# Last chunk of a gated state scan: key scaling, read-out sums, gates and the tensor engine's filler products change places

## The chip, the cores and the metric

The kernel runs on one core of a Trainium2 chip. The metric is the device time of one execution in microseconds (us). A core has a tensor engine (PE, with its weight loads shown apart as PEld), a vector engine (DVE), a scalar engine (ACT), GpSimd (POOL) and a queue engine for transfers (SP). Each takes its own instructions strictly in the order written; between engines only counting semaphores hold an instruction back.

## The reference

Four layers run on x of 4 rows (batch entries) by 1024 positions by 256 numbers, each followed by a residual sum and a layer norm: retention attention, a feed-forward block with four wide products, a gated state scan, and a small mixing layer. The change touches the scan and the mixing layer of the last chunk:

```python
# scan: for each position t, 32 blocks of 8; here the batch is the "step"
k_norm = k_t / (norm(k_t) + 1e-06)
retrieved = einsum('bnij,bnj->bni', S, k_norm)
S = tanh(S + outer(v_t - retrieved, k_norm))
Sq = einsum('bnij,bnj->bni', S, q_t)
out = Sq * silu(Sq)
# mixing layer
xr = mu_r * x + (1 - mu_r) * x_prev
xk = mu_k * x + (1 - mu_k) * x_prev
out = sigmoid(xr @ W_r.T) * (relu(xk @ W_k.T) ** 2 @ W_v.T)
```

The scan's first axis is what the other layers call the batch, so it has four steps (rows 0 to 3), each on 1024 positions that are independent of each other.

## The kernel before

The 1024 positions are cut into 8 chunks of 128, one position per partition. Attention runs first. Then a software pipeline (`schedule`) takes one chunk after another through the feed-forward layer, the scan of the chunk before and the mixing of the one before that. Behind it stands `finish()`, written once for each engine, with an order of instructions written out by hand: the last feed-forward product, the scan and mixing layer of the last chunk (number 7), and the mixing layer of chunk 6. `finish()` starts at about 1041 us of the profiled execution and is all that the change touches; nothing of it issues a transfer but the four stores at the end.

Names within `finish()`:

- A step's state is 128 partitions by 2048 numbers and is handled in two halves, (step, 0) and (step, 1), of 1024 numbers each.
- DVE: `guess_of(rows)` sums a row's squared keys (L2422) and makes a first guess of the inverse root. `scaled_keys(n, rows)` takes the reciprocal of the norm (L2436) and multiplies the keys (L2438). `next_state(s, hf)` computes state times keys (L2452), a sum (L2454), a difference (L2456), an outer product (L2458) and the added state (L2460). For the second halves of steps one and two, `state_delta` (L2467, L2471, L2473) and `state_added` (L2479) leave the outer product to POOL. `read_sum` (L2487) sums a product of state and query that POOL made; `last_read` makes that product on DVE (L2500) and sums it (L2502). `gate_rows` (L2529, L2532) gates the read-out and adds the residual for two rows, front (0 and 1) or back (2 and 3). `mixed_pair` (L2561, L2565) ends the mixing layer of a pair of rows.
- POOL: `key_root(n, rows)`, 13 small operations (L2084 to L2095), refines the inverse root. `read_q` (L2108) multiplies state and query, `outer_product` is L2116, `mix_weights` L2071, `added_mean` L2123 and `added_root` L2130, L2056 and L2058 (mean and inverse root of a layer norm, with sums from ACT).
- ACT: `key_value_row(b)` squares keys (L1818) and copies keys and values out of PSUM (L1821), `query_row(b)` copies the query (L1826) and frees the one PSUM bank of all queries. `state_tanh` is L1834, `gate_parts` L1839 and L1840, `add_rows` and `add_squares` L1847 and L1858, `scaled_rows` L1798, `turned_pair` L1867 and L1870, `key_acts` L1892 and L1894, `mix_gates` L1901.
- PE: the mixing layer runs on four pairs of rows, numbered 0 to 3: chunk 6 rows 0 and 1, chunk 6 rows 2 and 3, chunk 7 rows 0 and 1, chunk 7 rows 2 and 3. For each, `turn_pair` transposes the normalised rows (L1482) and `pair_products`, `mixed_gates` and `pair_values` are the products (L1257). `busy_while_waiting` (L1534) issues products whose result nobody reads.

Two chains matter here. The layer norm of rows 0 and 1 of chunk 7 is made from `gate_rows(front)` by `add_rows` on ACT, `added_mean` on POOL, `add_squares` on ACT, `added_root` on POOL and `scaled_rows` on ACT; `turn_pair(2, 0)` on PE waits for it. On ACT, `gate_parts(slice(3, 4), 8)`, which `gate_rows(back)` needs, stands behind `turned_pair(2, 0)`.

## Time and profile before

| | us |
|---|---|
| median of 3 runs | 1147.5 (1146.8 to 1147.91) |
| the profiled execution's own time | 1148.03 |
| its span, first to last instruction | 1146.2 |
| DVE's last instruction ends, from the span's start | 1143.5 |

Times inside the kernel are us from the start of the span. The profiled execution is 0.5 us above the median of the three runs, and 1.8 us of it lie outside the span. A timeline row gives the start, the length (several equal instructions in a row are merged, "x4"), the engine, the line, the operation and the tiles. A bracket says how long the engine had been idle before it and who released it. One product of 128x256 in fp32 leaves two records on PE, so "x16" there stands for 8 products; a transpose leaves one.

### The profile page before, as it was taken

The page shows a single profiled execution, that of the slowest core. Times are in us where ns is not written, and L with a number is a line of the kernel's source. Part 1 is how long each engine was busy: PE and PEld are TensorE (multiplying, and loading weights), DVE is VectorE, ACT ScalarE, POOL GpSimd, SP SyncE. Part 2 cuts the span into 40 slices and gives each one's busy share as a digit, 9 for nine tenths or more (in the row PEclk, how much of TensorE's full clock was granted, in tenths as well). Part 3 has the DMA queues.
Part 4 walks back from the last instruction along what each step waited for, and adds up shares of the span by engine and source line. Part 5 has one row for each costly group of instructions (what it writes and reads, how often), then busy time and mean ns, then how long its engine had stood idle before and what let it go on. Part 6 is the DMA issues. An engine that isn't in the chain of part 4 may idle for free.

```text
span 1146.2 us, 16629 instructions
## 1 busy us (share of the span) xinstructions
PE 1094.4 (95%) x5837; PEld 849.7 (74%) x5837; DVE 958.0 (84%) x1384; ACT 597.4 (52%) x1011; POOL 517.9 (45%) x426
## 2 busy tenths in 40 slices
PE   8999999999999999999999999999999999999286
PEld 4566666678787777788778887877887787887165
DVE  4798888882045998999899899989989998999997
ACT  2345555554446346645755574565557455644535
POOL 1477666774333244433424432443343344337852
PEclk9999999999999999999999999999999999999789
DMA  7247555523532430523134133314232330430001
GB/s 264 102 162 242 212 213 209 209 93 113 179 94 58 145 110 20 147 74 129 56 110 137 48 110 91 128 39 125 75 126 73 110 128 19 129 92 20 0 1 39
DMA packets 45114, 127.01 MB, mean 111 GB/s; under 512 B 4352, under 2 KB 21504, under 8 KB 43136
## 3 DMA queue, kind: packets, MB, share of 16 engines
q1 hardware_dynamic: 43904, 114.20, 31.4%
q10 hardware_dynamic: 1152, 12.07, 2.8%
q8 instruction: 33, 0.54, 0.2%
q14 instruction: 25, 0.20, 0.1%
HBM read 117.86 MB, written 19.92 MB: 120 GB/s over the span
## 4 chain that ended last, share of the span: by engine, by line
PE 76%; DVE 12%; POOL 6%; issue 3%; ACT 2%; DMA 0%; SPq 0%; POOLq 0%; DVEq 0%; ACTq 0%
PE lower L1257 46%; PE bank L1257 17%; PE lower L440 5%; PE lower L572 2%; POOL state L748 2%; POOL rgn L757 2%; PE bank L1246 1%; DVE y L847 1%; DVE y L852 1%; PE bank L487 1%; POOL a_lo L2026 1%; PE lower L526 1%; DVE tmp L2259 1%; DVE tmp L2273 1%; DVE Sq L2261 1%
## 5 line engine op out<-in xcount | busy, mean ns | idle before, releaser
L2026 POOL TENSOR_TENSOR a_lo<-whole,a_hi 128x512 fp32r<-128x512 f32 x128 | 182.0, 1440 | 266.9 <-ACT a_hi L1636 195.6
L1257 PE MATMUL lower<-b_hi,ring 128*128 128x512 f32 x512 | 193.6, 396 | 1.4 <-ACT a_hi L1636 1.4
L1257 PE MATMUL lower<-b_lo,ring 128*128 128x512 f32 x512 | 190.6, 390 | 1.7 <-POOL b_lo L2026 1.7
L1257 PE MATMUL lower<-a_hi,ring 128*128 128x512 f32 x496 | 186.3, 394 | 1.7 <-issue 1.7
L1257 PE MATMUL lower<-a_lo,ring 128*128 128x512 f32 x496 | 184.1, 389 | 0.3 <-POOL a_lo L2026 0.3
L2026 POOL TENSOR_TENSOR b_lo<-whole,b_hi 128x512 fp32r<-128x512 f32 x64 | 93.4, 1467 | 145.6 <-ACT b_hi L1636 145.6
L1619 ACT ACTIVATE S<-S 128x1024 f32<-128x1024 f32 x56 | 58.6, 1058 | 175.0 <-DVE S L2286 175.0
L1635 ACT ACTIVATE whole<-lower,hs 128x512 f32<-128x512 f32 x126 | 86.3, 685 | 79.2 <-PE lower L1257 79.1
L1257 PEld LDWEIGHTS lower<-b_hi,ring 128*128 128x128 f32 x512 | 96.2, 188 | 21.9 <-issue 1.8
L1257 PEld LDWEIGHTS lower<-b_lo,ring 128*128 128x128 f32 x512 | 96.0, 188 | 22.0 <-POOL b_lo L2026 2.3
L440 PE MATMUL lower<-wa,xT 128*128 128x512 f32 x240 | 109.3, 599 | 2.6 <-DVE turned L817 1.4
L1257 PEld LDWEIGHTS lower<-a_hi,ring 128*128 128x128 f32 x496 | 93.1, 188 | 21.2 <-issue 2.1
L1257 PEld LDWEIGHTS lower<-a_lo,ring 128*128 128x128 f32 x496 | 93.1, 188 | 19.8 <-POOL a_lo L2026 0.7
L2273 DVE TENSOR_TENSOR tmp<-S,kvq 128x1024 f32<-128x1024 f32 x42 | 80.5, 1916 | 1.4
L440 PEld LDWEIGHTS lower<-wa,xT 128*128 128x128 f32 x240 | 43.3, 190 | 50.0 <-issue 46.4
L2259 DVE TENSOR_TENSOR tmp<-S,kvq 128x1024 f32<-128x1024 f32 x56 | 75.9, 1355 | 0.7 <-ACT S L1619 0.7
L1257 PE MATMUL bank<-wkvq,wide_b 128*128 128x512 f32 (+1 forms) x200 | 68.1, 496 | 4.2 <-ACT kvq L1826 3.7
L2261 DVE TENSOR_REDUCE Sq<-tmp 128x128 f32<-128x1024 f32 x56 | 68.3, 1220 | 1.9
L1257 PE MATMUL lower<-w3r,a_hi 128*128 128x256 f32 x256 | 61.8, 283 | 1.3 <-ACT a_hi L1636 1.3
L1257 PE MATMUL lower<-w3r,a_lo 128*128 128x256 f32 x256 | 61.9, 283 | 1.0 <-POOL a_lo L2026 1.0
L1257 PEld LDWEIGHTS bank<-wkvq,wide_b 128*128 128x128 f32 x200 | 38.6, 195 | 32.2 <-issue 23.8
L2286 DVE TENSOR_TENSOR S<-S,tmp 128x1024 f32<-128x1024 f32 x42 | 57.3, 1364 | 1.4
(302 smaller groups left out, 2402.7 us busy)
## 6 DMA issues: line engine op xcount, KB each, us to landing
ring<-ffn_copy_dram SPq DMA_DIRECT2D x128, 512.0 KB, 3.6
look<-ffn_dram ACTq DMA_DIRECT2D x6, 1879.0 KB, 6.9
ffn_copy_dram<-ffn_dram SPq DMA_DIRECT2D x4, 2112.0 KB, 11.0
rope<-rope_dram SPq DMA_DIRECT2D x8, 512.0 KB, 8.2
xtok<-x_dram SPq DMA_DIRECT2D x8, 512.0 KB, 4.3
x1in<-x_dram SPq DMA_DIRECT2D x8, 512.0 KB, 4.8
x1res<-x_dram SPq DMA_DIRECT2D x8, 512.0 KB, 3.3
xT<-xT_dram SPq DMA_DIRECT2D x7, 512.0 KB, 8.8
```

The lines of the kernel that those rows point to most:

```text
L440: ins = nc.tensor.matmul(banks_of(n, b)[half][:], xT[:, parity, k, b, :], wa[:, k, half * 512:half * 512 + 512], start=(k == 0), stop=(k = ...
L572: ins = nc.tensor.matmul(bank[2 + b // 2][:, (b % 2) * DIM:(b % 2) * DIM + DIM], zT[:, k, b * P:b * P + P], wo[:, k, :], start=(k == 0), s ...
L748: nc.gpsimd.tensor_tensor(st, st, up_sum[:, b], ALU.add).then_inc(sum_done, 1)
L757: nc.gpsimd.tensor_tensor(rgn[:, rows].rearrange("p b h -> p (b h)"), var[:, rows].rearrange("p b h -> p (b h)"), inv_pow[:, 0:2 * HEADS], ...
L1257: ins = nc.tensor.matmul(out, a, b, start=(first and n == 0), stop=(last and n == len(pairs) - 1))
L1619: nc.scalar.activation(half, half, ACT.Tanh).then_inc(post_tanh, 1)
L1635: nc.scalar.activation(t["whole"][:, m % 4, :], bank_of(n, c)[:], ACT.Gelu, scale=scale).then_inc(act_done, 1)
L2026: nc.gpsimd.tensor_tensor(lo[:, m, :], t["whole"][:, m % 4, :], hi[:, m, :].bitcast(F32), ALU.subtract).then_inc(lo_done, 1)
L2259: steps.done(nc.vector.tensor_tensor(w, st, along_j(q), ALU.mult))
L2261: nc.vector.tensor_reduce(Sq[:, s, hf * HALF * BS:(hf + 1) * HALF * BS].rearrange("p (n i) -> p n i", i=BS), w, AX_X, ALU.add).then_inc(sq ...
L2273: scan.done(nc.vector.tensor_tensor(w, st, along_j(k), ALU.mult))
L2286: nc.vector.tensor_tensor(st, st, w, ALU.add).then_inc(pre_tanh, 1)
```

## The change

- DVE: `guess_of(slice(1, 2))` stands between the two halves of the last read-out of chunk 6 and not behind them. `scaled_keys(2, ...)`, the scaling of the keys of rows 2 and 3, stands inside `next_state(0, 1)`, between its sum and its difference, and not behind it. `read_sum(2, 1)` stands ahead of `gate_rows(front)`. The product of `(3, 0)` is made by `last_read(0)` on DVE; `read_sum(3, 0)` goes.
- POOL: `read_q(3, 0)` goes.
- ACT: `query_row(1)` and `key_value_row(2)` stand ahead of the two big activations of chunk 6's read-out, and the rows behind them are shifted by one. `turned_pair(1, 1)` stands ahead of `state_tanh(2, 1)`, `key_acts(1, 1)` ahead of `state_tanh(3, 0)`, and `mix_gates(1, 1)` ahead of `add_rows(1, ...)`.
- PE: in front of `turn_pair(2, 0)` it waits for `mean_done` 2, which is POOL's `added_mean(1)`, and then issues 18 unread products in place of 6; three more stand between `turn_pair(2, 0)` and `pair_products(2, 0)`.

```diff
-            READS = {(0, 0): 1, (0, 1): 2, (1, 0): 3, (1, 1): 4, (2, 0): 6, (2, 1): 7, (3, 0): 9}
+            READS = {(0, 0): 1, (0, 1): 2, (1, 0): 3, (1, 1): 4, (2, 0): 6, (2, 1): 7}
...
                     pe.wait_ge(pair_sig, 2)
-                    busy_while_waiting(pair_banks(2)[1], 6)
+                    pe.wait_ge(mean_done, 2)
+                    busy_while_waiting(pair_banks(2)[1], 18)
                     turn_pair(2, 0)
+                    busy_while_waiting(pair_banks(2)[1], 3)
                     pair_products(2, 0)
...
                     key_value_row(1)
+                    query_row(1)
+                    key_value_row(2)
                     act.wait_ge(sq_done, (d + 1) * 2 * BATCH)
                     sqf = Sq[:].rearrange("p b d -> p (b d)")
...
-                    query_row(1)
+                    query_row(2)
                     state_tanh(0, 0)
-                    key_value_row(2)
+                    key_value_row(3)
                     state_tanh(0, 1)
-                    query_row(2)
-                    key_value_row(3)
                     query_row(3)
...
+                    turned_pair(1, 1)
                     state_tanh(2, 1)
                     gate_parts(slice(0, 2), 4)
-                    turned_pair(1, 1)
+                    key_acts(1, 1)
                     state_tanh(3, 0)
-                    key_acts(1, 1)
+                    mix_gates(1, 1)
                     add_rows(1, x3, range(0, 2), fin_x3, 1)
-                    mix_gates(1, 1)
                     add_squares(1, x3, range(0, 2))
...
-                        if s and (s == BATCH - 1 or hf):
+                        if s and hf:
                             pool.wait_ge(fin_post, 2 * s + hf + 1)
...
                     outer_product(2)
-                    read_q(3, 0)
                     added_mean(1, front)
...
-                    def next_state(s, hf):
+                    def next_state(s, hf, meanwhile=None):
...
                         fin.done(nc.vector.tensor_reduce(dl, w, AX_X, ALU.add))
+                        if meanwhile:
+                            meanwhile()
                         fin.wait()
...
                     earlier_x3(0)
+                    guess_of(slice(1, 2))
                     earlier_x3(1)
-                    guess_of(slice(1, 2))
...
-                    next_state(0, 1)
-                    scaled_keys(2, slice(2, BATCH))
+                    next_state(0, 1, lambda: scaled_keys(2, slice(2, BATCH)))
...
                     read_sum(2, 0)
+                    read_sum(2, 1)
                     gate_rows(front, 2, 1)
                     state_added(2)
-                    read_sum(2, 1)
-                    read_sum(3, 0)
+                    last_read(0)
                     last_read(1)
```

DVE in `next_state(0, 1)` before; L2436 and L2438 are the key scaling, `bank7` holds the differences, `x1in` a product of state and query:

```order
L2452 TENSOR_TENSOR lower<-whole,kvq_0 128x1024
L2454 TENSOR_REDUCE bank7<-lower 128x128
L2456 TENSOR_TENSOR bank7<-kvq_0,bank7 128x128
L2458 TENSOR_TENSOR lower<-bank7,kvq_0 128x1024
L2460 TENSOR_TENSOR lower<-whole,lower 128x1024
L2436 RECIPROCAL norm_0<-norm_0 128x64
L2438 TENSOR_TENSOR kvq_0<-kvq_0,norm_0 128x2x256
L2487 TENSOR_REDUCE Sq_0<-x1in 128x128
L2487 TENSOR_REDUCE Sq_0<-x1res 128x128
```

The same place after (lines are those of the changed kernel):

```order
L2453 TENSOR_TENSOR lower<-whole,kvq_0 128x1024
L2455 TENSOR_REDUCE bank7<-lower 128x128
L2437 RECIPROCAL norm_0<-norm_0 128x64
L2439 TENSOR_TENSOR kvq_0<-kvq_0,norm_0 128x2x256
L2459 TENSOR_TENSOR bank7<-kvq_0,bank7 128x128
L2461 TENSOR_TENSOR lower<-bank7,kvq_0 128x1024
L2463 TENSOR_TENSOR lower<-whole,lower 128x1024
L2490 TENSOR_REDUCE Sq_0<-x1in 128x128
L2490 TENSOR_REDUCE Sq_0<-x1res 128x128
```

The reciprocal and the multiplication of the keys moved up by three instructions, into `next_state(0, 1)`.

DVE in step three before, from the first sum of step two's read-out (`x1in`, `x1res` are POOL's products of the two halves, `lower` is a product of DVE's own):

```order
L2487 TENSOR_REDUCE Sq_0<-x1in 128x128
L2529 SCALAR_TENSOR_TENSOR x3_0<-tmp_0 128x512
L2532 SCALAR_TENSOR_TENSOR x3_0<-x3_0,x2_0 128x512
L2479 TENSOR_TENSOR lower<-whole,S_0 128x1024
L2487 TENSOR_REDUCE Sq_0<-x1res 128x128
L2487 TENSOR_REDUCE Sq_0<-x1in 128x128
L2500 TENSOR_TENSOR lower<-whole,kvq_0 128x1024
L2502 TENSOR_REDUCE Sq_0<-lower 128x128
```

The same place after:

```order
L2490 TENSOR_REDUCE Sq_0<-x1in 128x128
L2490 TENSOR_REDUCE Sq_0<-x1res 128x128
L2532 SCALAR_TENSOR_TENSOR x3_0<-tmp_0 128x512
L2535 SCALAR_TENSOR_TENSOR x3_0<-x3_0,x2_0 128x512
L2482 TENSOR_TENSOR lower<-whole,S_0 128x1024
L2503 TENSOR_TENSOR lower<-whole,kvq_0 128x1024
L2505 TENSOR_REDUCE Sq_0<-lower 128x128
L2503 TENSOR_TENSOR lower<-whole,kvq_0 128x1024
L2505 TENSOR_REDUCE Sq_0<-lower 128x128
```

The sum over `x1res` moved ahead of the gates, and a product and its sum (L2503, L2505) stand where the second sum over `x1in` was.

PE from the gate products of pair 1 to those of pair 2 before (`bank5<-wv` are the value products of pair 1, L1482 with `x3_0` is `turn_pair(2, 0)`, with `x1in` `turn_pair(3, 1)`):

```order
L1257 MATMUL bank4<-mixw,x3T_0 128x256 x8
L1257 MATMUL bank5<-wv,wide_a_0 128x256 x4
L1534 MATMUL bank4<-wk,ident 128x256 x6
L1482 MATMUL bank6<-ident,x3_0 128x128 x4
L1257 MATMUL bank4<-x3T_0,mixw 128x256 x8
L1257 MATMUL bank5<-wr,wide_b_0 128x256 x4
L1482 MATMUL bank4<-ident,x1in 128x128 x4
```

The same place after:

```order
L1257 MATMUL bank4<-mixw,x3T_0 128x256 x8
L1257 MATMUL bank5<-wv,wide_a_0 128x256 x4
L1534 MATMUL bank4<-wk,ident 128x256 x18
L1482 MATMUL bank6<-ident,x3_0 128x128 x4
L1534 MATMUL bank4<-wk,ident 128x256 x3
L1257 MATMUL bank4<-x3T_0,mixw 128x256 x8
L1257 MATMUL bank5<-wr,wide_b_0 128x256 x4
L1482 MATMUL bank4<-ident,x1in 128x128 x4
```

The 6 unread products became 18, and 3 more stand behind the transposes.

## Rows read from the trace of the kernel before

**Rows 1.** Busy time by stage: us, each engine's busy us, PEclk granted clock

```profile
core 0: us, PE busy (x) PEld busy (x) DVE busy (x) ACT busy (x) POOL busy (x), PEclk, DMA share, GB/s
...
1110.60:1121.90 11.30, 8.25 (x38) 6.59 (x37) 11.21 (x10) 5.65 (x15) 6.97 (x6) 1.00 0.00 0
1121.90:1138.80 16.90, 15.38 (x64) 12.43 (x64) 12.28 (x44) 10.15 (x24) 3.03 (x5) 0.90 0.01 4
```

**Rows 2.** Chain of work that ended last, 1105 to 1146: start, us, what

```profile
1116.06 0.91 ACT x L1847 x4
...
1120.75 1.09 ACT x L1798 x2
...
1123.27 7.15 PE bank L1257 x24
```

**Rows 3.** Timeline of DVE, step one: start, us, engine, line, operation, [idle before <-releaser]

```profile
1061.10 1.22 DVE L2259 TENSOR_TENSOR tmp<-S,kvq 128x1024 f32<-128x1024 f32 x1
...
1070.74 0.69 DVE L2422 TENSOR_REDUCE norm<-y 128x64 f32<-128x512 f32 x1 [0.84 <-ACT y L1818]
...
1072.34 0.35 DVE L2436 RECIPROCAL norm<-norm 128x32 f32<-128x32 f32 x1 [0.45 <-POOL norm L2095]
...
1073.18 1.23 DVE L2452 TENSOR_TENSOR lower<-whole,kvq 128x1024 f32<-128x1024 f32 x1
```

**Rows 4.** Timeline of POOL, step one, key roots and first mean

```profile
1061.08 1.34 POOL L2093 TENSOR_TENSOR norm<-norm,newton 128x32 f32<-128x32 f32 x1
...
1064.41 0.24 POOL L2086 TENSOR_TENSOR newton<-root 128x32 f32<-128x32 f32 x1 [1.68 <-DVE root L2428]
...
1073.24 1.26 POOL L2123 TENSOR_SCALAR mean<-mv 128x4 f32<-128x4 f32 x1 [0.93 <-ACT x L1847]
```

**Rows 5.** Timeline of DVE, key scaling of rows 2 and 3, and its size unhindered

```profile
1084.29 2.70 DVE L2438 TENSOR_TENSOR kvq<-kvq,norm 128x512 f32<-128x512 f32 x1
1087.03 1.22 DVE L2487 TENSOR_REDUCE Sq<-x1in 128x128 f32<-128x1024 f32 x1
...
1106.56 0.68 DVE L2561 SCALAR_TENSOR_TENSOR y<-y,bank 128x512 f32<-128x512 f32 x1
```

**Rows 6.** Timeline of POOL beside it

```profile
1081.81 2.34 POOL L2108 TENSOR_TENSOR x1in<-whole,kvq 128x1024 f32<-128x1024 f32 x1
1084.11 2.34 POOL L2108 TENSOR_TENSOR x1res<-whole,kvq 128x1024 f32<-128x1024 f32 x1
1086.43 2.26 POOL L2071 TENSOR_SCALAR mixw<-wr,nu_r 128x256 f32<-128x256 f32 x2
```

**Rows 7.** Timeline of DVE, step three

```profile
1110.61 1.21 DVE L2487 TENSOR_REDUCE Sq<-x1in 128x128 f32<-128x1024 f32 x1
1111.74 1.53 DVE L2529 SCALAR_TENSOR_TENSOR x<-tmp 128x512 f32<-128x512 f32 x1
1113.30 2.72 DVE L2532 SCALAR_TENSOR_TENSOR x<-x 128x512 f32<-128x512 f32 x1
```

**Rows 8.** Timeline of POOL, step three

```profile
1112.68 2.80 POOL L2108 TENSOR_TENSOR x1in<-whole,kvq 128x1024 f32<-128x1024 f32 x1
1117.06 0.22 POOL L2123 TENSOR_SCALAR mean<-mv 128x2 f32<-128x2 f32 x1 [1.58 <-ACT x L1847]
```

**Rows 9.** Timeline of PE, mixing layer

```profile
1094.45 3.62 PE L1257 MATMUL bank<-mixw,x3T 128*128 128x256 f32 x16
1097.90 1.89 PE L1257 MATMUL bank<-wv,wide_a 128*128 128x256 f32 x8
...
1104.29 6.52 PE L1257 MATMUL bank<-x3T,mixw 128*128 128x256 f32 x16 [4.06 <-ACT x3T L1870]
...
1117.50 2.86 PE L1534 MATMUL bank<-wk,ident 128*128 128x256 f32 x12 [1.51 <-ACT y L1901]
1121.90 0.66 PE L1482 MATMUL bank<-ident,x 128*128 128x128 f32 x4 [1.54 <-ACT x L1798]
...
1130.24 0.60 PE L1482 MATMUL bank<-ident,x1in 128*128 128x128 f32 x4
```

**Rows 10.** Busy time by stage, PE's granted clock behind its idle time

```profile
1104.30:1110.00 5.70, 5.70 (x14) 4.53 (x15) 5.59 (x6) 1.02 (x1) 3.02 (x2) 0.50 0.01 3
```

**Rows 11.** Timeline of DVE, last norm of rows 2 and 3

```profile
1128.43 0.74 DVE L2539 TENSOR_SCALAR x1in<-x,mv,rstd 128x256 f32<-128x256 f32 x2 [0.81 <-POOL rstd L2164]
```

## The prediction

> **What bounds the kernel now.** Up to about 1061 us both kernels issue the same work, so everything below is about the last 85 us. I read the busy time by stage first: from 1110.6 to 1121.9 DVE is busy 11.21 of 11.30 us and so sets the pace, while from 1121.9 to 1138.8 it is busy 12.28 of 16.90 and PE 15.38 [rows 1]. So there are two regimes: DVE until the layer norm of rows 0 and 1 of chunk 7 has its input, then a hand-over chain. The chain of waits names the hand-over: sums on ACT at 1116.06, scaled rows at 1120.75, PE from 1123.27 [rows 2]. The two meet in one event, the transposes of pair 2, which start at 1121.90 [rows 9]. I call that moment the turn. The sum has two parts: when the turn comes, and how long it is from there to the end (1146.2 - 1121.9 = 24.3 us now). Only then come the timelines, for prices.
>
> **One mechanism sets many prices.** When DVE runs an instruction with two SBUF inputs and POOL an instruction, one waits for the other. The key multiplication took 2.70 us; an instruction of the same size took 0.68 [rows 5]. It began at 1084.29, behind POOL's product that had begun at 1084.11 and ended at 1086.45, and 1086.45 + 0.68 less some 0.15 of start-up is its end, 1086.99 [rows 5, 6]. The other way round, POOL's first mean, a matter of 0.22 us [rows 8], took 1.26 beside DVE's product at 1073.18 [rows 3, 4].
>
> **Step one.** DVE waits 0.84 us for row 3's squared keys and 0.45 for POOL's root of row 1 [rows 3]. With `query_row(1)` copied first, PE makes the later rows' keys without waiting for ACT's two big activations; with row 1's guess made one half earlier, POOL starts its root at about 1062 in place of 1064.41 [rows 4]. Both waits go: -1.29. What is late next is nothing; I see 0.1 to 0.2 us of slack behind each, and take -1.25. DVE's first product of step one is then at 1071.9.
>
> **Key scaling inside step one.** The multiplication now comes about 1.3 us ahead on DVE's own clock. POOL must first finish the root of rows 2 and 3 and three small instructions of the first norm; by the spacings of its rows its read product (1081.81 before) starts at about 1080.7, DVE's multiplication at 1080.15. So DVE goes first and pays 0.68 in place of 2.70: -2.02, and one dependency gap less, -0.1. It is not all kept. POOL's two read products now begin behind it and take 2 x 2.3 [rows 6], ending at 1085.5; DVE reaches the second sum at 1084.7 and waits 0.85, and its next product meets POOL's weight scaling (1.13 each of two) [rows 6] and loses 0.45. Net -0.8. Bounds: -2.1 if neither is met, 0 if POOL's product gets in first after all.
>
> **Step three.** DVE is 2.1 us early when it comes to its first sum, 1110.61 before [rows 7], 1108.5 now. Before, the two gate instructions took 1.53 and 2.72 [rows 7], held up by POOL's outer product and then by its read product of 2.80 us [rows 8]. Now the sum over `x1res` (1.13 from start to start) lies beside the outer product, and POOL's read product is gone, so both gates cost 0.68: 1.21 + 1.13 + 2 x 0.70 = 3.6 in place of 1116.02 - 1110.61 = 5.4, that is -1.8. The front gates end at 1112.1, 3.9 us early. The product that DVE takes over from POOL costs it 1.23 a little later; it lies in front of the back gates, which wait for the turn anyway (below), so at nothing, and 1.2 if that cover went.
>
> **The mean.** It starts 1.04 us behind the end of the front gates (1117.06 - 1116.02) [rows 7, 8], at 1113.1. There DVE has just begun, at 1113.1 as well, its new product with two SBUF inputs. Which goes first? At 1061.08 POOL began 0.02 us before DVE and still lost: it took 1.34 us, and DVE its normal 1.22 [rows 3, 4]. A lead of 0.18 won (1084.11 against 1084.29). I take DVE first and the mean done at 1114.4; with POOL first it is 1113.3. The Trainium skill (SBUF — State Buffer, section on the two separate sides) says that whichever of the two starts first has the shared pair for the whole instruction; by that rule the 0.01 us that POOL may be ahead would decide, and it would also have decided at 1061.08, where the trace disagrees.
>
> **PE's 18 products.** This term turns the sign. PE now waits for the mean and then issues 18 unread products before the turn. One costs 0.43 us: the 8 products at 1094.45 have the next behind them at 1097.90, 3.45 / 8 [rows 9], at full clock. 18 x 0.43 + 0.1 for the first = 7.9 us, so the turn is at 1114.4 + 7.9 = 1122.3 even at full clock, against 1121.90 now. Without them it would come when the rows are ready: mean to turn took 1121.90 - 1117.28 = 4.6 us, hence about 1119.0 to 1119.8. The 3.9 us won on DVE are spent on products that nobody reads. And PE is colder: pair 1 is ready earlier, so PE ends its last product at about 1110.5 and idles 3.9 us before the 18. After an idle time of 4.06 us its next products ran at half clock, 0.50 for 5.70 us, while after 1.51 us the clock stayed full, 1.00 over the stage [rows 1, 9, 10]. At half clock a product costs 0.86. From nought to 5.9 us of half clock are possible; between 3 and 7 products of the 18 then cost 0.43 more, 1.3 to 3.0. I take 3.6 products, the lower half, because the fall takes part of the idle time itself: +1.5. The turn: 1122.3 + 1.5 = 1123.8, that is +1.9.
>
> **Behind the turn.** The three extra products (1.3 us) lie beside ACT's copy of the transposed rows (1121.90 to 1123.27 now, 1.37), at nothing; unhidden they would cost 1.3. The products of pair 2 ran from 1123.27 to 1130.24 [rows 9], part of it at half clock; all at full clock they are 12 x 0.43 = 5.2, so PE would be 1.8 us earlier at the transposes of pair 3. But those also need rows from DVE, which were ready at 1129.17 [rows 11], 7.27 behind the turn, in place of PE's 8.34. So -1.07, and -0.3 at least if a little of the chain on DVE slips. I take -0.9. From pair 3 on the work is the same.
>
> **Other moves.** ACT's early copies of pair 1 make `state_tanh(2, 1)` about 1 us late; DVE reads it 5 us later. Pair 1's products end over 5 us early, which nobody awaits, its cost being the idle time above. No transfer is moved.
>
> **The sum.** DVE and POOL bring the mean 1117.28 - 1114.4 = 2.9 us forward; the 18 products take 7.9 + 1.5 where 4.6 were needed: +4.8; behind the turn -0.9. In all -2.9 + 4.8 - 0.9 = +1.0; with the half clock at 5 products +1.6. I take +1.3. Against the profiled execution's own 1148.03 that is 1149.3; it lay 0.5 above the median of 1147.5, so the median becomes 1148.8. About 0.2% (2.3 us) is what a measurement can tell from no change, so this is no change.
>
> **Rivals.**
> - *The mean slips in, and PE stays at full clock.* The turn is at 1113.3 + 7.9 = 1121.2, -0.7, and -0.9 behind it, of which 0.6 is lost to DVE's last read: -1.0 to 0, that is 1146.5 to 1147.5. For it speaks that POOL's start is not later than DVE's; against it 1061.08.
> - *Slower: a long half clock under the 18.* The place is PE from 1114.4. If PE's clock is already half and stays so for 5.9 us as at 1104.30 [rows 10], 7 products pay 0.43 more, 3.0, and the total is -2.9 + 3.3 + 3.0 - 0.9 = +2.5; each further product adds 0.43. It decides from 7 products at half clock on: 1150.0 to 1151. For it speaks that the idle time ahead is of the same length as the one that led there, against it that part of that time should be used up.
> - *Key scaling still loses to POOL.* The margin is about 0.5 us. Then 0.8 us of the gain goes: +2.1, 1149.6.
> - *Faster: the products are cover and no more.* If mean to turn took as long as the 18 (8 us, say by POOL's root and shift being held up by DVE's products at 1.2 us each), they would cost nothing beyond and the products behind them would be warm. But the hold-up can't exceed the 2.4 us of the two products, and it delays the turn itself, so the gain is at most the 3.9 us less that: 1144.5 to 1145.5. That asks for errors in two terms.
>
> **Chances.** Forecast 0.48; mean first and warm 0.20; scaling loses 0.07; slower 0.16; faster 0.09. Of the scaling case a fifth is over 2.3, of the forecast a little: slower 0.18, same 0.73, faster 0.09. The range leaves out the faster case and the tail of the slower one: 1146.6 to 1150.5.
>
> **What would show it.** The idle times of 0.84 and 0.45 on DVE gone; the key multiplication at 0.7 us and, behind it, an idle 0.8 before the second sum; gates of 0.7 us each; the mean 2.9 to 4 us earlier; 36 records of unread products over 8 to 11 us with the ACT row copy waiting for PE; the turn later than 1121.9 though its rows are ready by 1120; the products of pair 2 at full clock. Wrong would be: a turn before 1121, or an unread product that costs much less than 0.43.

## The result, and the profile after

| | before | after |
|---|---|---|
| median, us (20 runs of each) | 1147.07 | 1148.47 |
| lowest to highest | 1146.39 to 1148.01 | 1148.1 to 1149.83 |
| span of the profiled execution | 1146.2 | 1147.7 |

The ratio is 1.0012, with a 95% interval of 1.0007 to 1.0018: 1.4 us slower, inside the 0.2% that the forecast called no change, and 0.3 us below the forecast of 1148.8. The interval leaves out 1, so this is a small loss and not none. The 0.3 us come from the base: the forecast was +1.3 on a median of 1147.5 from three runs, and the 20 runs of before have theirs at 1147.07. Of the 20 times of after, 14 lie from 1148.1 to 1148.82 and six from 1149.23 to 1149.83; the profiled execution (1149.49) is one of the six, and that of before (1148.03) lies 1.0 above its median, so the two traces are a fair pair but neither is the median execution.

The common work ahead runs 0.27 us late in the trace of after (DVE's same product starts at 1058.97 in place of 1058.70); where two kernels are compared below, this is taken off or said. Line numbers of after are one to three higher than those of before.

Timeline of DVE after, step one and the key scaling, to be held against [rows 3, 5]:

```profile
1070.17 0.68 DVE L2423 TENSOR_REDUCE norm<-y 128x64 f32<-128x512 f32 x1
...
1071.22 0.34 DVE L2437 RECIPROCAL norm<-norm 128x32 f32<-128x32 f32 x1
...
1072.05 1.23 DVE L2453 TENSOR_TENSOR lower<-whole,kvq 128x1024 f32<-128x1024 f32 x1
...
1080.30 0.69 DVE L2439 TENSOR_TENSOR kvq<-kvq,norm 128x512 f32<-128x512 f32 x1
...
1085.69 1.22 DVE L2490 TENSOR_REDUCE Sq<-x1res 128x128 f32<-128x1024 f32 x1 [0.65 <-POOL x1res L2110]
1086.83 1.28 DVE L2453 TENSOR_TENSOR lower<-whole,kvq 128x1024 f32<-128x1024 f32 x1
```

The two idle times of step one are gone, the key multiplication took 0.69 us in place of 2.70, and the wait that took its place is the 0.65 in front of the second sum.

The same timeline in step three, for [rows 7], and POOL's mean beside it, for [rows 8]:

```profile
1108.21 1.21 DVE L2490 TENSOR_REDUCE Sq<-x1in 128x128 f32<-128x1024 f32 x1
...
1110.47 0.68 DVE L2532 SCALAR_TENSOR_TENSOR x<-tmp 128x512 f32<-128x512 f32 x1
1111.18 0.69 DVE L2535 SCALAR_TENSOR_TENSOR x<-x 128x512 f32<-128x512 f32 x1
...
1112.92 1.23 DVE L2503 TENSOR_TENSOR lower<-whole,kvq 128x1024 f32<-128x1024 f32 x1
```

```profile
1112.90 1.32 POOL L2125 TENSOR_SCALAR mean<-mv 128x2 f32<-128x2 f32 x1 [2.58 <-ACT x L1849]
```

The gates took 0.7 us each, and the mean, 0.02 us ahead of DVE's product, lost to it and took 1.32 us in place of 0.22.

Timeline of PE, for [rows 9], and of ACT, both after:

```profile
1114.37 10.55 PE L1534 MATMUL bank<-wk,ident 128*128 128x256 f32 x36 [4.03 <-POOL mean L2125]
1124.76 0.60 PE L1482 MATMUL bank<-ident,x 128*128 128x128 f32 x4
1125.20 1.46 PE L1534 MATMUL bank<-wk,ident 128*128 128x256 f32 x6
1126.50 3.62 PE L1257 MATMUL bank<-x3T,mixw 128*128 128x256 f32 x16
...
1132.00 0.66 PE L1482 MATMUL bank<-ident,x1in 128*128 128x128 f32 x4 [0.16 <-DVE x1in L2542]
```

```profile
1117.68 1.09 ACT L1800 ACTIVATE x<-x,shift,rstd 128x256 f32<-128x256 f32 x2 [1.42 <-POOL shift L2060]
...
1125.40 0.59 ACT L1872 COPY x3T<-bank 128x512 f32<-128x512 f32 x1 [5.93 <-PE bank L1482]
```

The rows of pair 2 were ready at 1118.8 (1117.68 + 1.09). The turn came at 1124.76: 6 us later, because PE was still on its 18 unread products. The chain of waits (start, us, what) has them as its longest piece behind 1105:

```profile
1114.37 10.55 PE bank L1534 x36
```

Busy time by stage after, for [rows 1, 10] (us, then PE, PEld, DVE, ACT and POOL busy, PE's granted clock, DMA share, GB/s):

```profile
1110.60:1121.90 11.30, 7.53 (x23) 6.27 (x24) 8.48 (x9) 4.70 (x14) 3.36 (x4) 0.70 0.00 0
1114.40:1119.20 4.80, 4.80 (x12) 3.81 (x12) 3.81 (x4) 3.38 (x9) 2.04 (x3) 0.50 0.00 0
1119.60:1124.80 5.20, 5.20 (x26) 4.53 (x25) 0.58 (x1) 0.00 (x0) 0.00 (x0) 1.00 0.00 0
```

DVE, busy 11.21 us of the first stage before, is busy 8.48 now. The first six or so unread products ran at half clock, the others at full. In the last row no engine but PE does anything to speak of: it is most of the time that the unread products cost.

### The profile page after: what moved, and what is told of

Same layout as the page of the kernel before. It is cut to its first block, busy times and chain, and to the rows that moved or that the text cites. A ratio compares the mean times of both kernels' runs of the same rounds, so it can differ in the third digit from the quotient of the medians.

```text
span 1147.7 us, 16690 instructions
## 1 busy us (share of the span) xinstructions
PE 1098.6 (96%) x5867; PEld 853.8 (74%) x5867; DVE 953.9 (83%) x1385; ACT 598.0 (52%) x1011; POOL 516.6 (45%) x425
## 4 chain that ended last, share of the span: by engine, by line
PE 77%; DVE 11%; POOL 7%; issue 3%; ACT 2%; POOLq 0%; DVEq 0%; ACTq 0%
PE lower L1257 46%; PE bank L1257 17%; PE lower L440 5%; PE lower L572 2%; POOL state L748 2%; POOL rgn L757 2%; PE bank L1246 1%; DVE y L847 1%; DVE y L852 1%; PE bank L487 1%; POOL a_lo L2028 1%; PE bank L1534 1%; PE lower L526 1%; DVE tmp L2274 1%; DVE tmp L2260 1%
```

## The experiments

The theory: DVE, POOL and ACT do win about 3 us, and PE's 18 products behind the mean take it back and more, because they are longer than what they wait beside. The rival: the unread products are cover that keeps the clock up and costs nothing, and the gain is lost elsewhere. All twelve kernels compute the whole result; only order, waits and unread products differ. Each table row gives the median, the ratio to the kernel before, timed beside it on the same chip, with its 95% interval, and from the profiled execution when the mean was done, when the turn came, and how far behind it the transposes of pair 3 started.

| kernel | median | ratio | mean | turn | to pair 3 |
|---|---|---|---|---|---|
| before | 1147.07 | 1 | 1117.28 | 1121.90 | 8.34 |
| after | 1148.47 | 1.0012 (1.0007 to 1.0018) | 1114.22 | 1124.76 | 7.24 |
| pe_alone | 1151.16 | 1.0037 (1.0024 to 1.0051) | 1117.62 | 1125.70 | 7.23 |
| rest_alone | 1145.84 | 0.9988 (0.9979 to 0.9997) | 1113.65 | 1118.24 | 9.77 |
| unread12 | 1145.69 | 0.9990 (0.9981 to 0.9999) | 1113.94 | 1120.77 | 7.22 |
| unread6 | 1143.81 | 0.9971 (0.9961 to 0.9982) | 1113.82 | 1119.22 | 7.23 |
| unread0 | 1145.91 | 0.9985 (0.9976 to 0.9994) | 1113.82 | 1118.62 | 9.93 |
| no_wait18 | 1143.53 | 0.9970 (0.9959 to 0.9981) | 1114.03 | 1118.62 | 7.32 |
| scaling_back | 1144.94 | 0.9983 (0.9974 to 0.9992) | 1115.38 | 1119.97 | 7.32 |
| step3_back | 1144.27 | 0.9978 (0.9969 to 0.9987) | 1114.29 | 1118.89 | 7.32 |
| step1_back | 1144.85 | 0.9979 (0.9970 to 0.9988) | 1115.77 | 1120.37 | 7.32 |
| pair1_back | 1147.04 | 0.9999 (0.9990 to 1.0008) | 1113.84 | 1121.84 | 7.23 |
| free16_with3 | 1141.93 | 0.9951 (0.9937 to 0.9965) | 1112.98 | 1116.94 | 7.45 |
| free16 | 1141.70 | 0.9951 (0.9937 to 0.9964) | 1112.75 | 1116.70 | 7.46 |

Beside them the kernel before took 1147.17 (`pe_alone`, `rest_alone`, `unread6`, `unread0`), 1147.11 (`no_wait18`, `unread12`, `scaling_back`, `step3_back`) and 1147.51 (`pair1_back`, `step1_back`, both `free16`). A difference of medians from two of these groups can be off by 0.4 us for that reason; where it matters, the one worked out from the ratios is given too.

**The two parts apart.** `pe_alone` is before with PE's part of the change, `rest_alone` is after without it:

```diff
                     pe.wait_ge(pair_sig, 2)
-                    pe.wait_ge(mean_done, 2)
-                    busy_while_waiting(pair_banks(2)[1], 18)
+                    busy_while_waiting(pair_banks(2)[1], 6)
                     turn_pair(2, 0)
-                    busy_while_waiting(pair_banks(2)[1], 3)
                     pair_products(2, 0)
```

(this is `rest_alone` against after; `pe_alone` is the same lines the other way round, against before)

> The kernel before with PE's part of the change alone: the wait for the mean, 18 unread products in place of 6 in front of the turn, 3 behind it. If the unread products stand on the path: the mean stays at 1117.3, 18 x 0.43 = 7.7 us and up to 1.5 of half clock put the turn at 1125.3 to 1126.8 in place of 1121.9, about 0.9 comes back behind it: +2.5 to +4 us, a ratio of 1.0022 to 1.0035. The rival, that they are cover which the path does not feel (the rows of pair 2 come late anyway, and a warm clock pays for them): 0 to -1 us.

> The changed kernel with PE's part as in the kernel before: 6 unread products, no wait for the mean, none behind the turn. The 6 then start at about 1110.5, behind pair 1, and are over before the mean is made at 1114.3. My theory: DVE, POOL and ACT bring the rows of pair 2 forward to 1118.8, the turn comes right behind them, at 1118.9 in place of 1121.9, and with the half clock of the idle PE in the products of pair 2 the end is 2 to 3 us earlier than the kernel before: a ratio of 0.9974 to 0.9983. The rival, that the end is set behind the turn by DVE and ACT, whose order of work is the same there: 0 to -1 us. The second rival, that PE's clock gives it all back: -0.5 to +0.5.

PE's part alone costs 4.0 us (1151.16 against 1147.17), the upper end of what the theory said, and the rest alone wins 1.3 (1145.84 against 1147.17), less than the 2 to 3 expected. The rival of `pe_alone` is out. Timelines of PE, `pe_alone` first:

```profile
1117.83 8.04 PE L1534 MATMUL bank<-wk,ident 128*128 128x256 f32 x36 [1.44 <-ACT y L1903]
```

```profile
1109.61 2.75 PE L1534 MATMUL bank<-wk,ident 128*128 128x256 f32 x12
1118.24 1.12 PE L1482 MATMUL bank<-ident,x 128*128 128x128 f32 x4 [5.88 <-ACT x L1798]
1120.04 6.41 PE L1257 MATMUL bank<-x3T,mixw 128*128 128x256 f32 x16 [0.68 <-ACT x3T L1870]
```

In `rest_alone` the rows are there 3.7 us earlier than before, the turn with them, as the theory says. But PE had then been idle for 5.88 us, and pair 2's products ran at half clock: 6.41 us for 16 records in place of after's 3.62, and 9.77 us to pair 3 in place of 7.24. The kernel before pays a part of this too, 8.34 to pair 3:

```profile
1123.27 5.41 PE L1257 MATMUL bank<-x3T,mixw 128*128 128x256 f32 x16 [0.72 <-ACT x3T L1870]
```

So of the 3.7 us at the turn 1.4 are lost again behind it, where the expectation (3.0 at the turn, 2 to 3 at the end) had left 0 to 1. That makes 2.3 in this pair of traces; the other 1.0 of the miss is the place of the two profiled executions, 0.9 above the median in before and 0.2 below it in `rest_alone`. A few unread products near the turn are worth their place (`unread6` below is 2.0 us faster than `rest_alone`); 18 behind the mean are not.

**How many.** After, with 6, 12 or none of the 18; the wait and the 3 stay:

```diff
                     pe.wait_ge(mean_done, 2)
-                    busy_while_waiting(pair_banks(2)[1], 18)
+                    busy_while_waiting(pair_banks(2)[1], 6)
```

> The changed kernel with 6 unread products in place of 18, the wait for the mean kept and the 3 behind the turn kept. They start at 1114.4 and last 2.6 us at full clock or 5.2 at half, so they end at 1117.0 to 1119.5, while the rows are ready at 1118.8. My theory: the turn moves from 1124.8 to 1118.9 to 1119.6; of these 5.2 to 5.9 us some 1 to 2 are lost to the half clock behind the turn: -3.5 to -4.5 against the changed kernel, a ratio to the kernel before of 0.997 to 0.998. The rival, that the products keep the clock full for what follows and pay for themselves: no change against the changed kernel, ratio 1.001.

> The changed kernel with 12 unread products in place of 18, the wait and the 3 kept. If each unread product behind the wait costs 0.43 us at full clock and the half clock lies under the first 5 to 6 of them: 12 take 7.7 us, the turn is at 1121.6 to 1122.0, 2.5 us behind the run with 6 and 2.6 us ahead of the changed kernel, the end the same: a ratio of 0.9988 to 0.9993. The rival, that fewer than 18 leave pair 2's products at half clock: the turn as said, but its products slower than 3.6 us for 16 records.

> The changed kernel with no unread product in front of the turn, the wait for the mean kept and the 3 behind the turn kept. PE stands idle from 1110.4 to 1118.8, all 8.4 us. My theory: the turn is at 1118.9, the 3 unread and the 8 products of pair 2 run at half clock for up to 6 us, the transposes of pair 3 come some 9 us behind the turn and not 7.2: -3 against the changed kernel, about 1 us worse than with 6, a ratio to the kernel before of 0.998 to 0.999. The rival, that the clock costs more than the products: 0 or slower against the changed kernel.

From 18 to 12 the median falls by 2.8 us and from 12 to 6 by 1.9, 0.39 for each of the 12 products (timed apart, with medians of before within 0.1 us); from 6 to none, on one chip, it rises by 2.1. The rival (no change) is out for `unread6`, which is 4.7 us faster than after and 3.4 faster than before. That is more than the 3.5 to 4.5 expected, for nothing was lost behind the turn (7.23 to pair 3); the loss from six to none, about 1 expected, was 2.1. PE in `unread6`, in `unread12` and in `unread0`:

```profile
1113.97 5.41 PE L1534 MATMUL bank<-wk,ident 128*128 128x256 f32 x12 [4.03 <-POOL mean L2125]
```

```profile
1114.08 6.85 PE L1534 MATMUL bank<-wk,ident 128*128 128x256 f32 x24 [4.03 <-POOL mean L2125]
```

```profile
1118.62 1.09 PE L1482 MATMUL bank<-ident,x 128*128 128x128 f32 x4 [8.68 <-ACT x L1799]
1119.50 2.77 PE L1534 MATMUL bank<-wk,ident 128*128 128x256 f32 x6
1122.06 4.93 PE L1257 MATMUL bank<-x3T,mixw 128*128 128x256 f32 x16
```

Six products took 5.41 us, all at half clock (0.50 over 1113.9 to 1119.2), and ended 0.9 us behind the rows, which were ready at 1118.37. Behind them the clock was full. With none, the turn is only 0.6 us earlier and the half clock falls on the work behind it. `unread12` came to its turn 0.8 to 1.2 us earlier than expected, since its half clock ended sooner: 0.50 up to 1117.0, then 1.00, while with the same idle time ahead after kept it to about 1119.5. It began later too: with PE idle since 1110.05 the clock fell between 1113.5 and 1113.75 in `unread12`, and between 1112.5 and 1112.75 in after, idle since 1110.34. Its rival is out, for pair 2's 16 records took 3.62 us there. Stages of `unread12`:

```profile
1114.10:1117.00 2.90, 2.90 (x7) 2.36 (x8) 1.95 (x2) 1.87 (x5) 1.69 (x3) 0.50 0.00 0
1117.00:1120.80 3.80, 3.80 (x19) 3.29 (x19) 2.82 (x4) 1.79 (x5) 0.35 (x1) 1.00 0.00 0
```

**The place, not the number.** After without the wait for the mean, 18 and 3 kept:

```diff
                     pe.wait_ge(pair_sig, 2)
-                    pe.wait_ge(mean_done, 2)
                     busy_while_waiting(pair_banks(2)[1], 18)
```

> The changed kernel without PE's wait for the mean; 18 unread products in front of the turn and 3 behind it stay. They now start right behind pair 1 at about 1109.8 and take 18 x 0.43 = 7.8 us, so they are over at 1117.6, before the rows of pair 2 are ready at 1118.4, and PE never stands idle long enough to lose its clock. If it is the place of the 18 behind the mean that costs the time: the turn is at 1118.4 to 1118.8 in place of 1124.8, the transposes of pair 3 follow 7.2 behind, and the end is some 5.5 us earlier than in the changed kernel and 0.5 to 1 earlier than with 6 behind the wait: a ratio to the kernel before of 0.996 to 0.9968. The rival, that the number of unread products costs, wherever they stand: no change against the changed kernel, 1.001.

It came out 4.9 us below after, so the rival is out. PE's timeline, and the stage up to the turn:

```profile
1109.98 7.93 PE L1534 MATMUL bank<-wk,ident 128*128 128x256 f32 x36
1118.62 0.66 PE L1482 MATMUL bank<-ident,x 128*128 128x128 f32 x4 [0.71 <-ACT x L1799]
```

```profile
1110.00:1118.00 8.00, 7.91 (x37) 6.63 (x35) 6.95 (x8) 3.43 (x11) 3.49 (x5) 1.00 0.00 0
```

The same 18 products start right behind pair 1, have no half clock, and are over 0.7 us before the rows. One wait is the whole difference to the changed kernel. Against `unread6`, though, `no_wait18` is only 0.3 us faster, not the 0.5 to 1 expected, and the two intervals overlap: these runs don't tell 18 without the wait from six behind it.

**The half clock and pair 1.** After, with ACT's part of pair 1 back where it was (PE's wait and 18 products kept):

```diff
-                    turned_pair(1, 1)
                     state_tanh(2, 1)
                     gate_parts(slice(0, 2), 4)
-                    key_acts(1, 1)
+                    turned_pair(1, 1)
                     state_tanh(3, 0)
-                    mix_gates(1, 1)
+                    key_acts(1, 1)
                     add_rows(1, x3, range(0, 2), fin_x3, 1)
+                    mix_gates(1, 1)
```

> The changed kernel, with ACT's copies, key activations and gates of pair 1 back where they were in the kernel before; all else as changed, the wait and the 18 products too. If it is the idle time of PE in front of the 18 (4.03 us, pair 1 being ready early) that puts their first six or so at half clock, then with pair 1 late again PE idles 4 us ahead of pair 1 instead, the half clock falls on pair 1's products, which nobody waits for, and the 18 take 7.9 us in place of 10.4: the turn is 1.5 to 2.5 us earlier than in the changed kernel, and the end with it, a ratio to the kernel before of 0.9990 to 1.0000. The rival, that the half clock has nothing to do with that idle time: no change against the changed kernel, 1.0012.

The median is 1.4 us below after (1147.04 against 1148.47); each held against before beside it, the difference is 1.9 (-0.5 and +1.4). The expectation was 1.5 to 2.5, so the lower end of it. The mean is done at the same time (1113.84, and 1113.86 in after with its later start of 0.36 taken off), so what moved the turn is PE: by 2.9 us, 2.5 with the 0.36 off. This pair of traces shows the difference large, since the profiled execution of `pair1_back` (1146.53) is one of its shorter ones and that of after one of its longer ones. PE's timeline, and two stages of it:

```profile
1101.51 5.41 PE L1257 MATMUL bank<-x3T,mixw 128*128 128x256 f32 x16 [2.30 <-ACT x3T L1872]
...
1113.99 8.01 PE L1534 MATMUL bank<-wk,ident 128*128 128x256 f32 x36 [1.90 <-POOL mean L2125]
```

```profile
1102.40:1105.60 3.20, 3.20 (x9) 2.52 (x8) 3.13 (x5) 1.02 (x1) 2.13 (x1) 0.50 0.02 5
1113.90:1121.80 7.90, 7.81 (x36) 6.91 (x37) 4.87 (x5) 3.77 (x10) 2.04 (x3) 1.00 0.00 0
```

With pair 1 late, the half clock lies under pair 1's products, for which nobody waits, and the 18 take 8.01 us, not 10.55. The idle time ahead of pair 1 was 2.30 us and not the 4 expected; the clock fell all the same, 0.8 us after its products had begun. The change made pair 1 early for no one, and paid for it in front of the turn.

**The parts on DVE, one by one.** Three kernels undo one part each, under a PE part in which the turn follows the mean: `scaling_back` and `step3_back` against `unread6`, `step1_back` against `no_wait18`. In `step3_back` the two lines of the change's diff that count and order POOL's read products (`READS` and the wait in `read_q`) go back too.

```diff
-                    next_state(0, 1, lambda: scaled_keys(2, slice(2, BATCH)))
+                    next_state(0, 1)
+                    scaled_keys(2, slice(2, BATCH))
```

> The changed kernel with 6 unread products, and the scaling of the keys of rows 2 and 3 back behind the first step's second half. The multiplication then meets POOL's read product and takes 2.3 to 2.7 us in place of 0.69. By the prediction's term 0.8 us of this reaches the mean, by what is seen in the changed kernel (0.05 lost at the next product in place of 0.45) 1.2 to 1.3: the mean, the turn and the end are 0.8 to 1.3 us later than with 6 unread products and the scaling inside. The rival, that the second sum waits for POOL anyway and nothing is won: 0.

```diff
...
                     outer_product(2)
+                    read_q(3, 0)
                     added_mean(1, front)
...
-                    read_sum(2, 1)
                     gate_rows(front, 2, 1)
                     state_added(2)
-                    last_read(0)
+                    read_sum(2, 1)
+                    read_sum(3, 0)
```

> The changed kernel with 6 unread products, and step three as in the kernel before: POOL makes the read product of (3, 0), the gates stand ahead of the sum over x1res, and the added product on DVE goes. My theory: the two gates take 1.5 and 2.7 us again, so the front gates end 1.8 us later, but POOL's mean takes 0.22 in place of 1.32, for no DVE product lies beside it: the mean is done 0.6 to 0.7 us later and so is the end. The rival, that the held-up mean costs nothing that the path feels (then all of the 1.8 shows): +1.8. A second rival, that the gates' gain never reached the path: 0.

```diff
                     key_value_row(1)
-                    query_row(1)
-                    key_value_row(2)
...
+                    query_row(1)
-                    query_row(2)
                     state_tanh(0, 0)
-                    key_value_row(3)
+                    key_value_row(2)
                     state_tanh(0, 1)
+                    query_row(2)
+                    key_value_row(3)
...
-                    guess_of(slice(1, 2))
                     earlier_x3(1)
+                    guess_of(slice(1, 2))
```

> The kernel without the wait and with 18 products, and the edits of step one undone: the query of row 1 is copied behind the two big activations and the guess of row 1 stands behind both halves of the read-out. If the two idle times on DVE (0.84 and 0.45 us) are what the edit removed, they come back, POOL's small operations are met otherwise, and the mean, the turn and the end are 1.2 to 1.4 us later than without this undoing: a ratio to the kernel before of 0.998 to 0.9985. The rival, that the later waits (DVE waits 0.64 for POOL's second read product) swallow it: 0.6 to 0.8.

The medians rise by 1.1, 0.5 and 1.3 us, by the ratios by 1.4, 0.8 and 1.0. Each was timed on another chip than the kernel it is held against, and the intervals overlap, so the traces are the sharper evidence. With the scaling back the mean is 1.27 us later (1.56, less the 0.29 by which step one's first product is late there), with step three back 0.65 (counted from the first sum of step three, 1114.29 - 1107.63 against 1113.82 - 1107.81), with step one back 1.94 (1.74, and 0.20 by which the common work is early there). DVE with the scaling back, then PE of the same kernel:

```profile
1083.06 2.71 DVE L2439 TENSOR_TENSOR kvq<-kvq,norm 128x512 f32<-128x512 f32 x1
```

```profile
1106.05 5.41 PE L1257 MATMUL bank<-mixw,x3T 128*128 128x256 f32 x16 [1.88 <-DVE y L2564]
...
1115.53 2.83 PE L1534 MATMUL bank<-wk,ident 128*128 128x256 f32 x12 [2.35 <-POOL mean L2125]
1119.97 0.66 PE L1482 MATMUL bank<-ident,x 128*128 128x128 f32 x4 [1.62 <-ACT x L1800]
```

The multiplication took 2.71 us again, so the rival (nothing won) is out. The turn moved by only 0.75 (0.46 with the 0.29 off), for here the half clock fell on pair 1's products and the six unread ones took 2.83 us in place of 5.41: in this pair of executions PE's clock gave most of the loss on DVE back before the turn.

With step three back, gates and mean are as before, and the 1.8 us on the gates shrink to 0.65 at the mean:

```profile
1108.76 1.53 DVE L2533 SCALAR_TENSOR_TENSOR x<-tmp 128x512 f32<-128x512 f32 x1
1110.33 2.71 DVE L2536 SCALAR_TENSOR_TENSOR x<-x 128x512 f32<-128x512 f32 x1
```

```profile
1114.07 0.22 POOL L2125 TENSOR_SCALAR mean<-mv 128x2 f32<-128x2 f32 x1 [1.58 <-ACT x L1849]
```

That settles the two rivals: not 1.8, since the mean's hold-up gives 1.1 back, and not 0.

With step one back, DVE waits once, for 1.92 us, and PE, idle for 3.75 until ACT copies the query, makes the later keys partly at half clock. DVE and PE of `step1_back`, and PE before:

```profile
1071.72 0.69 DVE L2422 TENSOR_REDUCE norm<-y 128x64 f32<-128x512 f32 x1 [1.92 <-ACT y L1819]
```

```profile
1065.82 6.31 PE L1257 MATMUL bank<-wkvq,wide_b 128*128 128x256 f32 x12 [3.75 <-ACT kvq L1827]
```

```profile
1065.91 5.23 PE L1257 MATMUL bank<-wkvq,wide_b 128*128 128x256 f32 x12 [3.75 <-ACT kvq L1826]
```

The prediction had priced this edit by DVE's two idle times alone. It is worth 1.9 us in this pair of traces, 1.4 between before and after (1073.18 to 1072.05, and 0.27), and 1.3 in the medians, and part of it is PE's clock: these products took 5.23 us in one execution and 6.31 in the other. The rival of 0.6 to 0.8 is out by the trace; the medians alone, 1.0 by the ratios, would not exclude it.

**A version that beats both.** No wait, 16 products, and on DVE the first instruction of pair 1's mixing (its second input is a PSUM bank) ahead of the product of (3, 0). Against after:

```diff
-                    pe.wait_ge(mean_done, 2)
-                    busy_while_waiting(pair_banks(2)[1], 18)
+                    busy_while_waiting(pair_banks(2)[1], 16)
                     turn_pair(2, 0)
-                    busy_while_waiting(pair_banks(2)[1], 3)
...
                     state_added(2)
+                    mixed_bank(1, 1)
                     last_read(0)
                     last_read(1)
-                    mixed_pair(1, 1)
+                    mixed_sum(1, 1)
```

`mixed_bank` and `mixed_sum` are the two instructions of `mixed_pair`; `free16_with3` keeps the 3 behind the turn.

> The kernel without the wait, with 16 unread products in front of the turn and 3 behind it, and on DVE the first instruction of the mixing of pair 1, whose second input is a PSUM bank, in the place behind the added state, ahead of the product of (3, 0). POOL's mean then meets no DVE instruction with two SBUF inputs. My theory: the mean takes 0.22 us in place of 1.32, the rows of pair 2 are ready 1.1 to 1.5 us earlier, at 1117.1, the 16 products are over at 1117.0, the turn is at 1117.2, and the end 1.0 to 1.4 earlier than with 18 and no wait: a ratio of 0.9958 to 0.9962. The rival, that DVE's own work up to the back gates (its five large instructions behind the added state end at 1118.3) is the bound: 0.2 to 0.5 earlier.

> The same without the 3 unread products behind the turn. PE starts the products of pair 2 when ACT's copy is over, about 0.5 us earlier, but the transposes of pair 3 wait for DVE's rows in either. If the 3 cost nothing, as the prediction says: no change against the same kernel with them, within 0.3 us. The rival, that PE is the later of the two: 0.5 us faster.

`free16` takes 1141.7 us, a ratio of 0.9951 (0.9937 to 0.9964): 5.8 us faster than before and some 7 faster than after (6.8 by medians not timed side by side, 7.0 by the ratios). `free16_with3` was expected 1.0 to 1.4 us ahead of `no_wait18` and came 1.6 ahead, 2.2 by the ratios. DVE and POOL in `free16`:

```profile
1112.54 0.68 DVE L2562 SCALAR_TENSOR_TENSOR y<-y,bank 128x512 f32<-128x512 f32 x1
1113.14 1.22 DVE L2501 TENSOR_TENSOR lower<-whole,kvq 128x1024 f32<-128x1024 f32 x1
1114.39 1.22 DVE L2503 TENSOR_REDUCE Sq<-lower 128x128 f32<-128x1024 f32 x1
```

```profile
1112.52 0.23 POOL L2123 TENSOR_SCALAR mean<-mv 128x2 f32<-128x2 f32 x1 [2.58 <-ACT x L1847]
1113.95 0.45 POOL L2130 TENSOR_SCALAR mv<-mv 128x2 f32<-128x2 f32 x1 [1.21 <-ACT S L1858]
...
1115.30 0.20 POOL L2058 TENSOR_TENSOR shift<-rstd,mean 128x2 f32<-128x2 f32 x1
```

The mean is as close to a DVE instruction as in after (0.02 us ahead), but that one reads one input from PSUM, and the mean takes 0.23 us. The shift, 1.11 or 1.12 in the other kernels, takes 0.20, for it now stands beside DVE's sum (L2503, one input) and not beside a product; the expectation had not counted this gain. The small instruction at 1113.95 still meets the product at 1113.14 and takes 0.45 in place of 0.19. The Trainium skill (SBUF — State Buffer, section on who interferes with whom) says that a DVE instruction with at most one SBUF input, outside the modes that use two ports, does not contend with GpSimd; by that rule the mean and the shift had to come out so, and the trace agrees. The rival, that DVE's own work is the bound, is out, though only just: DVE waits 0.19 for ACT in front of the back gates. PE without the 3 waits 0.66 us for DVE's rows:

```profile
1124.16 0.66 PE L1482 MATMUL bank<-ident,x1in 128*128 128x128 f32 x4 [0.66 <-DVE x1in L2540]
```

With them it still waits, 0.35. So the 3 cost nothing, as predicted: the ratios are the same, and both kernels need 7.45 us from the turn to pair 3.

## Why the prediction was right

- **Step one.** Predicted: both idle times go, first product at 1071.9. Trace: 1072.05, or 1071.8 with 0.27 taken off, a gain of 1.40 where 1.25 was taken. Right; what was missing is that DVE's wait hangs on PE's clock too (`step1_back`).
- **Key scaling.** DVE goes first and pays 0.69: right, as is the wait that replaces it (0.65 for 0.85). The 0.45 lost at the next product was 0.05 (1.28 for 1.23). Net 1.27 in place of 0.8, in after against before (1110.61 to 1107.94, less the 1.40 of step one) as in `scaling_back`: a term mis-sized by half a us. Why POOL's weight scaling hindered so little was not tested.
- **Step three.** Gates 0.68 and 0.69, front gates ended at 1111.9, 1111.6 with the 0.27 taken off (1112.1 said; the key scaling had won more). From the first sum to the end of the gates 3.66 us, for 3.6 said. The terms as written, 1.21 + 1.13 + 2 x 0.70, add up to 3.74; the first of them should have been 1.13 from start to start as well. Right but for this slip.
- **The mean.** DVE first, though POOL was 0.02 ahead, done at 1114.22, 1113.95 with the 0.27 off (1114.4 said). What held it up was no semaphore but DVE's product beside it. Right, and `free16` shows the mechanism by removing it. Each of the kernels with this order had the same 1.32.
- **The 18 products.** This step carried the sign, and it was right: they are on the path from end to end. At full clock they take 7.9 to 8.0 us, as worked out. The half clock was mis-sized: 1.5 us taken, 10.55 - 7.93 = 2.6 measured in the profiled execution, with six products at half clock and not 3.6. The prediction let the fall use up part of the idle time; it did, but enough was left to last until about 1119.5. In `unread12`, with the same idle time in front, the term came to 1.6 (6.85 less 12/18 of 7.93), so either size occurs. The profiled execution of after is one of its six longer ones; the other 14 are shorter by 1.2 us in the middle, which the 1.5 of the prediction would fit, but none of them was profiled, so this is not shown.
- **Behind the turn.** 7.24 us to pair 3 in place of 8.34, a gain of 1.1 where 0.9 was taken. The products ran at full clock and DVE's rows became the later of the two (0.16 us of wait), as said.
- **The sum.** With the offset of 0.27 taken off: mean -3.3 (-2.9 said), mean to turn +5.9 (+4.8), behind -1.1 (-0.9), together +1.5 for +1.0 worked out and +1.3 taken. Two gains a little larger and one loss larger by 1.1 met; that the median came within 0.3 us owes something to this.
- **The rivals.** "Mean slips in, PE at full clock" failed in both halves. "A long half clock" was nearest: six products at half clock, one short of where it begins (the 5.9 us that it takes from [rows 10] are 5.7 there). "Key scaling still loses" fell with the 0.69 us. "Products are cover and no more" fell with `no_wait18` and `unread6`. The idle time of PE, made by ACT's early pair 1, was in the forecast as the 1.5 of half clock, and `pair1_back` shows it as a cost of its own: 1.4 us by the medians, 1.9 against before.

## What to carry to other kernels

Filler products for the clock are to end when the data is ready. 18 of them behind a semaphore of the chain cost 4.9 us against the same 18 without the wait; six behind it ended 0.9 us behind the rows and did about as well as those; six that were over 5.9 us before the turn (`rest_alone`) left PE to fall to half clock and were 2.0 us slower. Without the wait many products are safe so long as they end in time; behind it a few too many go straight into the result. Work moved earlier on one engine is worth only what its reader can use, and can open an idle gap that makes the next products run at half clock. When a small operation on POOL stands on the path, put beside it a DVE instruction that reads at most one input from SBUF.

## What the runs showed of the hardware

- The price of the same idle time varies. Behind 4.03 us of idle PE the half clock cost 2.6 us in after and in `unread6` (5.41 - 2.83), and 1.6 in `unread12`; the same products of step one took 5.23 and 6.31 us. The Trainium skill (TensorE: Matmul & The Clock Gate, part on the clock gate) says of the start of a kernel that the number of products that run cold changes from run to run; the traces show the same in the middle of one, in kernels that are alike up to there. The times of a kernel that hangs on such a place spread more: 1146.38 to 1148.47 in `pair1_back`, 1143.32 to 1143.65 in `no_wait18`, whose PE kept full clock from 1098 to 1128. That the one causes the other fits but was not tested.
- The idle time directly ahead does not tell alone whether the clock falls. It fell behind 1.88 us (`scaling_back`, pair 1) and 2.30 us (`pair1_back`, pair 1), both times some 0.8 us after PE had begun to work again, and stayed full behind 2.35 us (`scaling_back`, the six unread products) and 1.90 us (`pair1_back`, the 18).
- A longer idle time did not cost much more: behind 5.88 and 8.68 us of it the way from the turn to pair 3 took 9.77 and 9.93 us in place of 7.2 to 7.3, that is 2.5 to 2.7 us, about what 4.03 us of it cost in after and `unread6`.
- Being 0.02 us ahead in the records does not let POOL go first against DVE: it was held up so at 1061.08 before, at 1112.90 after, and in the eight other traces in which the mean met the product.
